# A recurrence step: the reciprocal of the softmax sum made by GpSimd as a power of minus one, and DVE's weighted sums begun without it

## The reference, cut to what matters

```
def step(h, x_t):
    hid = jnp.broadcast_to(h[:, None, :], (Bn, Sn, Hn))
    combined = jnp.concatenate([hid, enc_hiddens], axis=2)
    score = jnp.tanh(jnp.einsum('bsk,kh->bsh', combined, W_att))
    score = jnp.einsum('bsh,h->bs', score, V_att[:, 0])
    attn = jax.nn.softmax(score, axis=-1)
    context = jnp.einsum('bs,bsh->bh', attn, enc_hiddens)
    inp = jnp.concatenate([x_t, context], axis=1)
    gz, gr, gh = jnp.split(inp @ Wi + b, 3, axis=1)
    rz, rr, rh = jnp.split(h @ Uh, 3, axis=1)
    z = jax.nn.sigmoid(gz + rz)
    r = jax.nn.sigmoid(gr + rr)
    hh = jnp.tanh(gh + r * rh)
    h_new = z * h + (1.0 - z) * hh
    return (h_new, h_new)
```

## Time and profile before

| | us |
|---|---|
| median of 3 runs | 4440.73 |
| lowest, highest | 4435.77, 4452.31 |
| the profiled execution's own time | 4437.57 |
| its span, first to last instruction | 4435.8 |

### The profile page before, as it was taken

One profiled execution on the slowest core, in us unless ns is written; L12 is line 12 of the kernel. 1 busy time (PEld: TensorE's weight loads), 2 busy tenths in 40 slices (PEclk: granted clock), 3 DMA queues, 4 the chain that ended last, 5 costly groups with the idle time before them and its releaser, 6 DMA issues. The chain is left out here.

```text
span 4435.8 us, 67916 instructions
## 1 busy us (share of the span) xinstructions
PE 3725.5 (84%) x19244; PEld 2085.3 (47%) x19244; DVE 2758.7 (62%) x13500; ACT 2299.3 (52%) x6560; POOL 656.7 (15%) x2307
## 2 busy tenths in 40 slices
PE   7888888888888888888899999678888888888768
PEld 2366666666666666666433334223333333333222
DVE  3457777777777777777534543556666666666534
ACT  5356666666666666666433334135555555555433
POOL 0322222222222222222320000310000000000002
PEclk9999999999999999999999999578888888888879
DMA  0100000000000000000110000011111111111000
GB/s 9 57 1 1 1 1 1 1 1 1 1 1 1 1 1 1 1 1 1 36 38 1 1 1 3 26 64 46 61 48 57 48 62 47 61 47 46 26 27 5
DMA packets 48773, 93.56 MB, mean 21 GB/s; under 512 B 11296, under 2 KB 31792, under 8 KB 48144
## 3 DMA queue, kind: packets, MB, share of 16 engines
q1 hardware_dynamic: 48400, 89.22, 6.2%
HBM read 72.88 MB, written 15.39 MB: 20 GB/s over the span
## 5 line engine op out<-in xcount | busy, mean ns | idle before, releaser
L2249 ACT ACTIVATE t_ex<-ps 128x1024 f32<-128x1024 f32 (+1 forms) x480 | 472.1, 1021 | 574.6 <-PE ps L2196 561.1
L922 PE MATMUL ps<-g_dh,w_p 128*128 128x77 f32 x2032 | 453.0, 304 | 353.1 <-DVE g_dh L1013 353.1
L930 PE MATMUL ps<-g_dh,w_p 128*128 128x128 f32 x4064 | 662.6, 285 | 0.0
L2344 DVE TENSOR_REDUCE t_ncol<-ps 128x1 f32<-128x512 f32 x768 | 486.4, 682 | 155.1 <-PE ps L2169 154.6
L922 PEld LDWEIGHTS ps<-g_dh,w_p 128*128 128x128 f32 x2032 | 302.1, 188 | 547.6 <-DVE g_dh L1013 547.6
L987 DVE SCALAR_TENSOR_TENSOR g_used<-g_encg,g_e 128x77 f32<-128x77 f32 x3072 | 550.0, 229 | 0.0
L930 PEld LDWEIGHTS ps<-g_dh,w_p 128*128 128x128 f32 x4064 | 535.1, 191 | 0.0
L939 PE MATMUL ps<-g_th,g_vrep 128*128 128x77 f32 x2048 | 453.9, 303 | 0.0
L957 ACT ACTIVATE g_th<-ps 128x77 f32<-128x77 f32 x1024 | 242.4, 237 | 384.3 <-PE ps L922 384.3
L934 PE MATMUL ps<-g_dh,g_uhh 128*128 128x129 f32 x2032 | 437.0, 297 | 0.0
L996 DVE TENSOR_REDUCE g_ntop<-ps 128x1 f32<-128x77 f32 x1024 | 243.0, 237 | 248.2 <-PE ps L939 196.8
(11 more groups left out here) (483 smaller groups left out, 5482.3 us busy)
## 6 DMA issues: line engine op xcount, KB each, us to landing
t_qst<-t_turn_q SPq DMA_DIRECT2D x288, 96.0 KB
t_kst<-t_turn_k SPq DMA_DIRECT2D x144, 96.0 KB
t_turn_q<-t_part SPq DMA_DIRECT2D x24, 384.0 KB, 2.5
t_turn_k<-t_part SPq DMA_DIRECT2D x12, 384.0 KB, 3.3
t_wf<-in_t_wf SPq DMA_DIRECT2D x6, 514.5 KB, 5.6
m_experts<-in_experts SPq DMA_DIRECT2D x1, 3072.0 KB, 12.3
t_wa<-in_t_wa SPq DMA_DIRECT2D x6, 448.0 KB, 3.5
t_wx<-in_t_wx SPq DMA_DIRECT2D x6, 448.0 KB, 4.4
```

The costliest lines, as they stand in the source:

```text
L922: M(att[c], w["att_h"], moved(c, t, S), start=False, stop=True, skip_group_check=True).then_inc(*st.sem("att", c))
L930: return M(gates[c][:, g], w["uh"][:, g * D:(g + 1) * D], moved(c, t, SPAN), start=False, stop=False, skip_group_check=True)
L2249: A(ex[0:kw, slot[pf, c, l, n]], ps[0:kw, at:at + 2], ACT.Exp, scale=SCALE).then_inc(*st.sem(f"{pf}e{n}", c))
L2344: V.tensor_reduce(ncol[:, c, n % TT, n // TT:n // TT + 1], ps[:, at], AX, ALU.max, negate=True)\
```

## The change

DVE no longer makes the reciprocal. POOL makes it, as `esum` to the power of minus one, with a column of minus ones as second input, in a new first operation `invert` ahead of `factor`. DVE's `mix` begins its weighted sums when the exponentials are there, and waits for `sinv` only before `zr`.

```diff
--- before.py
+++ after.py
@@ -816,7 +816,7 @@
         encp = sb("encp", [P, B, S])
         encg = sb("encg", [P, 3, B, S])
         identb = sb("identb", [P, P], BF16)
-        zero = sb("zero", [P, 1])
+        zero, minus = sb("zero", [P, 1]), sb("minus", [P, 1])
         uhh = sb("uhh", [P, D])
         vrep = sb("vrep", [P, P])
         hist = sb("hist", [P, B, T + 1])
@@ -832,7 +832,7 @@
 
         with ExitStack() as pctx:
             pre = Steps(k, "gpre", 2, pe="encp c0 c1 c2 g0 g1 g2", dve="encp_s c0_s c1_s c2_s")
-            ev = Steps(k, "gev", 1, dve="gx0 gx1 gx2", act="ax0 ax1 ax2", pool="h0 warm identb uhh vrep0 vrep1 zero")
+            ev = Steps(k, "gev", 1, dve="gx0 gx1 gx2", act="ax0 ax1 ax2", pool="h0 warm identb uhh vrep0 vrep1 minus zero")
             block = pctx.enter_context(nc.Block())
 
             @block.tensor
@@ -874,6 +874,7 @@
                 for c in range(B):
                     nc.gpsimd.tensor_copy(vrep[:, 64 * c:64 * c + 64], w["v"].broadcast_to([P, 64])).then_inc(*ev.sem(f"vrep{c}"))
                 pool.wait_ge(*ev.at("vrep1"))
+                nc.gpsimd.memset(minus[:], -1.0).then_inc(*ev.sem("minus"))
                 nc.gpsimd.memset(zero[:], 0.0).then_inc(*ev.sem("zero"))
                 pool.wait_ge(*ev.at("zero"))
 
@@ -900,7 +901,7 @@
         plain = [ps[:, 4 * c + 2, 3 * SPAN:3 * SPAN + 1] for c in range(B)]
 
         st = Steps(k, "g", 2, pe="att score gates", act="tanh exp tzr cand",
-                   dve="top sinv r z hm zr in dh", pool="omz h")
+                   dve="top r z hm zr in dh", pool="sinv omz h")
         summed = k.semaphore("g_summed")
         with nc.Block() as block:
             @block.tensor
@@ -997,10 +998,10 @@
 
                 def mix(c, t):
                     dve.wait_ge(*st.at("exp", c, t))
-                    V.reciprocal(sinv[:, c:c + 1], esum[:, c:c + 1]).then_inc(*st.sem("sinv", c))
                     weigh("r", 1, c)
                     weigh("z", 0, c)
                     weigh("hm", 2, c)
+                    dve.wait_ge(*st.at("sinv", c, t))
                     dve.wait_ge(*st.at("z", c, t))
                     dve.wait_ge(*st.at("gates", c, t))
                     fma("zr", c, zr[:, c], mac[:, c, 0:2], sinv[:, c:c + 1], gates[c][:, 0:2, t % SPAN])
@@ -1031,6 +1032,10 @@
 
             @block.gpsimd
             def _(pool):
+                def invert(c, t):
+                    pool.wait_ge(*st.at("exp", c, t))
+                    nc.gpsimd.tensor_tensor(sinv[:, c:c + 1], esum[:, c:c + 1], minus[:], ALU.pow).then_inc(*st.sem("sinv", c))
+
                 def factor(c, t):
                     pool.wait_ge(*st.at("tzr", c, t))
                     nc.gpsimd.tensor_scalar(omz[:, c:c + 1], tzr[:, c, 0:1], -0.5, 0.5, ALU.mult, ALU.add).then_inc(*st.sem("omz", c))
@@ -1042,6 +1047,7 @@
 
                 for t in range(T):
                     for c in range(B):
+                        invert(c, t)
                         factor(c, t)
                         advance(c, t)
                 for c in range(B):
```

## The result

| | median us | runs | against before |
|---|---|---|---|
| before, in the same comparison | 4439.77 | 4 | |
| the change | 4636.27 (4625.38 to 4641.46) | 4 | 1.0442, 95% interval 1.0422 to 1.0462 |
| forecast | 4412, range 4394 to 4570 | | |

What follows compares the result with a forecast made beforehand. It took the recurrence's step, 3.68 us, as bound by the latency of one lane's own chain. Of 0.08 us gained, 0.05 stayed after the queue's wait; 512 x 0.05 = 26 us off 4437.57 gave 4412 us, range 4394 to 4570.

Steps and rivals of the forecast that it cites:

- The 0.08 that goes: On DVE, dropping the reciprocal lets the first weighted sum start 0.08 us earlier each step, 41 us over 512 steps.
- A: The end of the exponentials' accumulator in a lane's step; the prediction counts the later starts from it.
- The queue's wait: Before the gates' sum, z's wait moves into DVE's queue: 0.49 after the first sum against 0.46, leaving 0.05 of 0.08.
- I take D = 0.34: D is the duration of POOL's 128x1 power, estimated at 0.34 us; up to 0.40 it was to cost nothing.
- The bounds, 0.19 and 1.26: Limits for the power's duration: POOL's 128x1 addition, 0.190 us, and its addition of 512 columns, 1.264 us.
- rival 3: Shared port makes POOL's power wait for the third weighted sum: 4545 us, or 4468 without 0.15 of arithmetic; chance 0.14.
- gates' sum at A + 0.12 + D: When the gates' sum on DVE can start if it waits for POOL's power; without that wait, A + 0.52.
- rival 2: A long power on POOL sets the gates' sum, deciding from D = 0.45: 4540 us at 0.65, 4855 at 1.264; chance 0.22.
- This isn't paid each step: a late lane 0 shifts against lane 1: In POOL's queue lane 0's power starts 0.11 late behind lane 1's h; the lanes shift, costing 0.1 us once.
- The rest of the kernel is untouched: Outside the recurrence, nothing was to change in time.
- the last h: Trace row at 2136.4: beside DVE's first addition into x, h took 0.56 us instead of 0.19; cited for a shared port.
- the h that wasn't held: Trace row at 1179.44: h began 0.09 after a first sum, still took 0.19 us; cited against a shared port.

Runs made afterwards that it cites:

- Run 1: The change with an addition in place of the power on POOL, so the softmax isn't divided by its sum: 4439.60 us, 0.9999 of before.
- run 7: Run 1 with the gates' sum waiting for z first, then sinv, so POOL's wait stands in the queue: 4416.49 us, 0.9957 of before.
- run 3: The change with the exponentials in PSUM, so the weighted sums read only one input from SBUF: 4526.54 us, 1.0202 of before.
- Run 8: The change with both each lane's power ahead of the other lane's h and the exponentials in PSUM: 4510.88 us, 1.0160 of before.
- run 2: The change with POOL's order altered, each lane's power ahead of the other lane's h: 4533.06 us, 1.0216 of before.
- run 10: The change with one more DVE wait per lane and step, for something long done: 4559.55 us, 1.0263 of before.
- run 4: The kernel before, keeping DVE's reciprocal, with the same powers also made on POOL into a column nobody reads: 4440.06 us, 1.0015 of before.
- run 5: Run 1 with one more DVE wait per lane and step, for something long done, ahead of the maximum: 4423.30 us, 0.9966 of before.
- run 9: The change with one idle POOL addition of 0.19 us ahead of each power: 4885.10 us, 1.0996 of before.

## Why the prediction was wrong

- **The 0.08 that goes.** Right in kind: the first sum starts at A + 0.03. Of the 0.08 the forecast kept 0.05. Run 1 kept 0.026 in the step, and the pauses on DVE took back those 13 us. The queue's wait was priced rightly (0.03, run 7); missing were the pauses, and the 0.02 that the second sum comes later when the first starts straight from a wait. It stays in run 3, where the sums have one SBUF input (0.16), so it isn't contention with POOL.
- **"I take D = 0.34".** This term was mis-sized: the power takes 0.55 alone and 0.56 in the change. The bounds, 0.19 and 1.26, did hold it; no row and no run shows the 0.34, or the 0.15 of arithmetic that rival 3 took from it: the choice of the value "nearer to the addition of the same shape" had nothing behind it. With the prediction's own formula, gates' sum at A + 0.12 + D, 0.56 gives A + 0.68, 0.11 a step, 4495: rival 2, and slower. So this term alone turned the forecast round, though not out of its range. Run 8, at A + 0.67, came to 4511, and run 2, with the power held to 0.60, to 4533; some 17 and 25 us of these are single long steps beyond those of before, which the formula doesn't have.
- **"This isn't paid each step: a late lane 0 shifts against lane 1".** This is the step that failed and took the time out of the range, and it is worth more than the first: 103 us between the change and run 2. The argument looked at each lane's chain by itself and gave the lanes room to shift. But POOL's order ties them both ways: lane 0's power behind lane 1's h, and lane 1's power behind lane 0's h. When lane 0 shifts away from lane 1's h, lane 1 comes nearer to lane 0's. The two distances add up to a loop, and once around it is a lower bound of the step that no shift of the lanes can pay off: 2 x 2.02 us with h held, 3.80 without (run 10). The trace of before had every link of it but D: from the candidate tanh to the update 0.39, to h 0.30, h itself 0.19, D + 0.03, and 0.49 from the gates' sum to the other lane's candidate tanh, 1.40 + D for half a step. At D = 0.34 that is 1.74, under the 1.84 of before, and rightly no concern; at 0.56 it is 1.96, 3.92 for the step. By these links it decides from D = 0.44, about where D itself begins to cost. (In fact POOL begins the power some 0.045 before h has ended. With that, the power's 0.55 and 0.48 for the last link, half the loop is 1.90, the 3.80 of run 10's short kind; the held h adds 0.10 to each half and the power and the last link 0.01 each, the 4.04.)
- **Rival 3, the shared port.** As it was priced it is wrong: the power doesn't wait for the third sum. It starts at A + 0.08 in run 2 and loses 0.05 (0.60 against 0.55), as much as a POOL instruction of 0.19 us that starts as far behind a first sum (0.235, an h of run 1); the two sums behind cost it nothing. But its mechanism is real in a place where it wasn't looked for, h. That takes 0.29 when it starts with the first sum, and ends 0.05 after it. All ten traces with both inputs of the sums in SBUF follow one rule: an h that starts with a sum or while one runs ends at the later of 0.19 after its own start and 0.05 after that sum's end. It holds for all 2645 such h within 0.005 us, and an h that starts 0.006 or more ahead of a sum takes 0.19. The prediction had two of the rows: the last h, held until 0.04 after an addition, and the h that wasn't held. It read the second as evidence against the first. But that h started 0.09 behind the sum, so its own 0.19 ended at 1179.63, and 0.05 after the sum's end is 1179.62: there was nothing left to hold.
  The Trainium skill, "SBUF — State Buffer", section "Who interferes with whom", has it that two such instructions exclude each other for the whole of the instruction. Where the sum starts first the traces agree, by the rule above: the h that starts together with it is held until it has ended (0.29, and 0.19 in run 3 with one SBUF input). Where the GpSimd instruction starts first they don't: an h 0.04 ahead of the sum delays it by nothing (the sum keeps its 0.24 us, run 10), and a power 0.04 ahead of it by only 0.02 to 0.03 (run 4).
- **The rest of the kernel is untouched.** Right, within 5 us.
- **The range and the chances.** 0.37 for slower was given, but no rival joined the long power with the queue behind it. A power at 0.56 was inside the range; the loop and the held h took the time 66 us beyond its upper end.

Summed up by differences of medians, from before to the change: a POOL operation of 0.19 us in place of the reciprocal 0 (run 1); the power's length in the lane's own chain with POOL's better order +93 (run 2); the order of POOL's queue, with the h that the first sum holds, +103. Of these 103 the hold is all, in the sense that either cure alone takes them away: at h = 0.19 the loop is 3.80, no longer than the lane's chain. In the traces the recurrence's growth of 204 us divides so, by the median step and by what single steps add to it: -13 and +13, +85 and +11, +122 and -14.

**What stays open.** Why DVE pauses at multiples of 128 instructions, and why only some of these places show it. Why the loop goes from one kind to the other: in run 10 it enters the long kind only at a long step (10 and 29 of every 64, two of the places where run 5 has its long steps too, and after 127, 255 and 383, long in every kernel) and leaves it at 15 and 47 of every 64, without one. That the long kind keeps itself up (the exponentials then start right behind the other lane's candidate tanh, 0.25 after its start, which makes h and the first sum coincide) is argued from the timeline, not tried. Why run 9 was granted a lower clock. And why a sum isn't held by an h that starts ahead of it, as the h is held by the sum.

## What to carry to other kernels

Before work is moved to another engine's queue, write down the loops that its order closes over all lanes, not only each lane's chain: what stands behind what, with durations, once around; half of such a loop is paid twice a step. A function on GpSimd that no row of the trace shows should be timed alone first, since its distance to an addition of the same shape can be a factor of three. And where one instruction per step comes or goes, a change of 15 us in a recurrence of 512 steps may be no more than where DVE's pauses fall, which shows as a mean step that moved otherwise than the median one.

## What the runs showed of the hardware that was not expected

- A power of 128x1 on POOL takes 0.548 us, an addition of the same shape 0.19. Two dependent waits at its ends cost 0.08 to 0.09 (ACT's end to POOL's start) and 0.03 (POOL's end to DVE's start).
- DVE pauses for some 0.3 us at places that are multiples of 128 instructions of its queue apart, waits counted. With 26 a step one step in 64 is long (before), or three (run 5), with 24 two in 16 (run 1): 13 to 16 us of 1881.
- A weighted sum of 77 columns is followed by the next after 0.145 us when another instruction ran ahead of it, and after 0.164 when it started from a wait.
- A POOL instruction of 0.19 us that starts together with a DVE instruction of two SBUF inputs ends 0.05 after it, at 0.29; the same holds for one that starts while it runs, if its own 0.19 would be over sooner. One that starts 0.006 or more ahead takes 0.19. In run 10 the two kinds of step differ by 0.04 us in this start and by 0.24 in length.
